# One more 512-column product on TensorE in the first 30 slots of each first attention

## What is computed

```python
def reference(...):
    x = L0_attn_x                                   # (4, 512, 128)
    x = _layernorm(x + _L0_attn_ref(x, ...))        # differential attention, 16 heads of width 8
    x = _layernorm(x + _L0_ffn_ref(x, ...))         # gated feed-forward of width 352, FP4-quantised
    x = _layernorm(x + _L1_attn_ref(x, ...))        # causal attention, 16 query / 4 key heads of width 64
    x = _layernorm(x + _L1_ffn_ref(x, ...))         # one of 8 experts for each token, width 512
    return x
```

```python
a1 = softmax(q1 @ k1.T * scale);  a2 = softmax(q2 @ k2.T * scale)
out = (a1 - lam * a2) @ v
```

## Time and profile before

| | |
|---|---|
| median of 3 runs | 1262.83 us (1258.26 to 1266.27) |
| the profiled execution | 1266.14 us |
| its span, first to last instruction | 1264.3 us |
| mean granted clock of TensorE | 0.843 of 2.4 GHz |
| TensorE (PE), matmuls | 1021.1 us busy, 81% |
| VectorE (DVE) | 786.8 us, 62% |
| ScalarE (ACT) | 641.5 us, 51% |
| GpSimd (POOL) | 424.9 us, 34% |
| DMA | 56.83 MB, 45 GB/s on average |

### The profile page before, as it was taken

One profiled execution on the slowest core, in us unless ns is written; L12 is line 12 of the kernel. 1 busy time (PEld: TensorE's weight loads), 2 busy tenths in 40 slices (PEclk: granted clock), 3 DMA queues, 4 the chain that ended last, 5 costly groups with the idle time before them and its releaser, 6 DMA issues.

```text
span 1264.3 us, 20021 instructions
## 1 busy us (share of the span) xinstructions
PE 1021.1 (81%) x7121; PEld 520.7 (41%) x7121; DVE 786.8 (62%) x1785; ACT 641.5 (51%) x1581; POOL 424.9 (34%) x512
## 2 busy tenths in 40 slices
PE   2588846889999878999988887999988847998754
PEld 1122321233455332455445442355444447455544
DVE  4789347983777678760787667862577562467431
ACT  1177612776266344677167434686257514257423
POOL 3000020300776304000776502200485630487411
PEclk7578955899999875799999775799999968999957
DMA  5300063000013000320103000230100005100052
GB/s 154 96 3 3 10 184 59 2 2 11 0 35 76 1 2 9 125 86 10 31 26 93 1 1 2 83 106 32 32 1 10 1 6 209 32 1 10 1 192 63
DMA packets 54305, 56.83 MB, mean 45 GB/s; under 512 B 13688, under 2 KB 46016, under 8 KB 53440
## 3 DMA queue, kind: packets, MB, share of 16 engines
q1 hardware_dynamic: 53184, 53.47, 14.3%
q0 software_dynamic: 1024, 2.10, 0.6%
HBM read 43.16 MB, written 16.20 MB: 47 GB/s over the span
## 4 chain that ended last, share of the span: by engine, by line
PE 50%; DVE 21%; ACT 10%; issue 8%; POOL 4%; DMA 4%; SPq 3%; POOLq 0%; ACTq 0%; DVEq 0%
PE ps L1583 8%; DVE mx L969 8%; PE ps L1566 5%; PE ps L1612 5%; PE ps L1625 5%; PE ps L1645 4%; PE ps L1655 4%; PE ps L1404 3%; PE ps L1500 3%; ACT PROB L1261 2%; PE ps L1415 2%; PE ps L1398 2%; PE ps L1541 2%; ACT PROB L1303 2%; DMA qst<-mrow 2%
## 5 line engine op out<-in xcount | busy, mean ns | idle before, releaser
L969 DVE TENSOR_REDUCE mx<-ps 128x1 f32<-128x512 f32 x512 | 323.7, 684 | 90.3 <-PE ps L1541 88.1
L1261 ACT ACTIVATE PROB<-ps 128x512 f32<-128x512 f32 x512 | 276.6, 602 | 166.1 <-PE ps L1566 164.4
L577 POOL TENSOR_SCALAR PROB<-PROB,rsum 128x128 f32<-128x128 f32 (+3 forms) x224 | 229.8, 1038 | 72.4 <-DVE rsum L1102 72.0
L1303 ACT ACTIVATE PROB<-ps,mx 128x128 f32<-128x128 f32 (+3 forms) x256 | 133.1, 527 | 165.6 <-DVE mx L1097 163.9
L1583 PE MATMUL ps<-PROB,v 128*32 128x256 f32 x2048 | 184.2, 452 | 3.0 <-ACT OREG L1270 2.6
L1541 PE MATMUL ps<-kst,qst 24*128 24x512 bf16 x512 | 158.9, 477 | 34.1 <-DVE mx L969 26.6
L1566 PE MATMUL ps<-qst,kst 27*128 27x512 bf16 x512 | 142.3, 450 | 39.3 <-ACT PROB L1261 22.8
L558 POOL CAST mparts<-mx 128x16 bf16<-128x16 f32 x32 | 7.0, 218 | 449.4 <-DVE mx L969 427.1
L1097 DVE TENSOR_REDUCE mx<-ps 128x1 f32<-128x128 f32 (+3 forms) x256 | 113.0, 483 | 64.4 <-PE ps L1628 64.2
L1645 PE MATMUL ps<-cst,PROB 128*128 128x128 f32 x640 | 114.2, 298 | 38.5 <-ACT PROB L1318 13.5
L1625 PE MATMUL ps<-MREG,QREG 64*128 64x384 f32 (+3 forms) x512 | 106.9, 495 | 0.0
(11 more groups left out here) (217 smaller groups left out, 1379.6 us busy)
## 6 DMA issues: line engine op xcount, KB each, us to landing
wexp<-expert_rows SPq DMA_DIRECT2D x44, 514.0 KB, 5.2
qk_terms<-RREG SPq DMA_DIRECT2D x48, 128.0 KB, 2.1
kst<-qk_terms SPq DMA_DIRECT2D x16, 192.0 KB
qst<-qk_terms SPq DMA_DIRECT2D x16, 192.0 KB
RREG<-sorted_x SPq DMA_DIRECT2D x4, 704.0 KB, 4.7
sorted_y<-RREG SPq DMA_DIRECT2D x4, 704.0 KB, 3.9
expert_rows<-in_L_ffn_W_dram SPq DMA_DIRECT2D x1, 2048.0 KB
expert_rows<-in_L_ffn_W_dram SPq DMA_DIRECT2D x4, 512.0 KB
```

The source lines that it names most:

```text
L577: pool.tensor_scalar(tile, tile, rsum1[:, 2 * v + half:2 * v + half + 1], None, ALU.mult).then_inc(scaled1, 1)
L969: dve.tensor_reduce(mx0[:, ga % 2, col:col + 1], ps[:, max_bank(k, MAX_SLOT[n]), :], AX, ALU.max, negate=True).then_inc(slot0_free, 1)
L1261: act.activation(prob0[:, s % 2, q % 4, q % 8 // 4], ps[:, s0_banks[q % len(s0_banks)], :], ACT.Exp, scale=float(HD0) ** -0.5).then_inc(ex ...
L1303: act.activation(prob1[:, half, at:at + w], ps[:, a1_bank(v, half), 0:w], ACT.Exp, bias=mx1[:, col:col + 1], accum_out=sum1[:, col:col + 1 ...
```

## The change

TensorE's program gets a helper, called once at the head of each slot of a stretch with a first attention. It issues one bfloat16 product: the identity as weights, 512 columns of the mask table as the moving operand, into bank 7. Nobody reads the result, and no semaphore is incremented. For r = -1 and 0 it does so in slots -8 to 25 (34 slots), for r = 1 and 2 in slots -4 to 25 (30 slots), so 128 times in all. For r = -1 the first of them waits for `rem_ready`, for r = 0 for `hid_done`, since bank 7 is in use before.

```diff
+            def keep_warm(s, c, r):
+                n = 4 * s + c
+                if not (-8 if r <= 0 else -4) <= n < 26:
+                    return
+                if r == 0 and n == -8:
+                    pe.wait_ge(hid_done, NT)
+                if r < 0 and n == -8:
+                    pe.wait_ge(rem_ready, 2)
+                pe.matmul(ps[:, 7, :], identb, pick.rearrange("p a m n -> p (a m n)")[:, 0:T], start=True, stop=True)
+
             def overlap(r):
                 k, i = r + 1, r - 1
                 s0_banks = score_banks(r)
                 ns = len(s0_banks)
                 for s, c in steps(r):
                     if k < BATCH:
+                        keep_warm(s, c, r)
                         if 0 <= s < 16:
                             g = s // 2
```

## The result

| | before | changed |
|---|---|---|
| median of 22 runs | 1265.94 us (1258.26 to 1270.69) | 1269.90 us (1264.90 to 1273.40) |
| span of the profiled execution | 1264.3 us | 1264.9 us |
| mean granted clock in it | 0.843 | 0.866 |

The ratio is 1.0035, with a 95% interval of 1.0024 to 1.0046: slower by 4.4 us (3.0 to 5.8), well within 1%. The forecast was 7.3 us slower. The two profiled executions differ by 0.6 us only; the one of the changed kernel ran in 1266.7 us, 3 us under its median. The runs of the kernel before spread over 12 us and those of the changed one over 9, so single stretches are compared in the profiles and whole times by the ratios.

What follows compares the result with a forecast made beforehand. No single bound: VectorE's maxima pace lead and 2.4 GHz slots, TensorE the 1.2 GHz slots with scores and values. Terms 2.0 - 1.7 + 1.6 + 2.2 + 3.0 + 0.9 - 0.4 - 0.6 + 0.3 = +7.3 us: 1270, range 1254 to 1283.

Steps and rivals of the forecast that it cites:

- The price of a product: On TensorE, per added product: 0.22 to 0.32 us at 2.4 GHz, taken as 0.27; 0.44 to 0.54 at 1.2, taken as 0.50.
- The lead and slots 0 to 5 hidden: Batches 0 and 1, 28 products hidden under VectorE's 1.20 us a slot: cost 0, at most 14 us if cover failed.
- Cold slots 6 and 7: First slots with values at 1.2 GHz, two each in batches 0 and 1: 4 x 0.50 = 2.0 us; 2.05 instead of 1.55 each.
- The clock of batch 0: Clock rises by 68 us and stays up to 95; five slots of batches 0 and 1 turn warm, -1.7 us.
- The warm slots of batches 0 and 1: 30 slots already at 2.4 GHz: product hidden in 0.31 us of slack, except about 6 with two sets of values, 1.6 us.
- The wait for `hid_done`: r = 0, slot -8: VectorE starves 1.1 us, the maxima row's DMA absorbs 1.0; taken as 0.3 us.
- Slots -3 to 0 of batches 2 and 3: Warm and bound by TensorE, one unbroken chain of output and maxima products: 8 x 0.27 = 2.2 us.
- Slots 9 and 11: Batches 2 and 3: with slot 14, three products a batch on the chain after a wait for VectorE, 6 x 0.50 = 3.0 us.
- The last run, half warm: Batches 2 and 3, TensorE's throughout, six slots a batch, half turning warm: 6 x 0.50 - 6 x 0.35 = 0.9 us.
- The reasoning on busy time: Busy time alone doesn't decide TensorE's clock; a whole-array product in each slot should tip unbroken runs of values.
- rival B: Faster: clock held through the whole last run of batches 2 and 3, -6.5 and -5 us; sum -8, 1255 us; chance 0.14.
- Rival A: Products fill TensorE's queue but its clock stays as it was: +17.6 us, so 1280; chance 0.24.

Runs made afterwards that it cites:

- the late products alone: Only the 26 products in slots 13 to 25 of batches 2 and 3, against the kernel before: 0.9961 (0.9935 to 0.9986), -4.9 us.

## Why the prediction was right, and where it was not

The time was forecast at +7.3 us and came at +4.4 (3.0 to 5.8), on the same side and in the range. Step by step:

- *The price of a product*, 0.50 and 0.27 taken out of 0.44 to 0.54 and 0.22 to 0.32. Measured on the chain behind the values: 0.54 and 0.32, the upper bounds, so the weight load adds its 0.10 us there. Behind L1415 in slots -3 to 0: 0.22, the lower bound. Right in kind; what stands in front decides which end holds.
- *The lead and slots 0 to 5 hidden.* Right: +1.4 us for 28, with an interval that includes none. Slots -8 to 0 of batch 0 took 11.23 us for 11.06. The lead of batch 0 kept its pace.
- *Cold slots 6 and 7.* Forecast 2.05 us each. Measured 2.10 and 2.08 from the reduction of slot 6 to that of slot 8, which hold the products of slots 7 and 8. In batch 0 three cold products paid (slots 6, 7 and 8), not two; in batch 1 the same window took 3.32 us for 3.11, at a clock of 0.72 for 0.50.
- *The clock of batch 0.* It was to rise by 68 us; it rose at 72, when L1594 falls to 0.57 us on the chain. Before, it had risen at about 71, so the products didn't bring the rise forward, and slot 8 was not won. The clock stayed up from then on, and slots 14 to 20 went from 9.52 to 8.64 us at 1.00. That the products did this isn't shown: they took 8.63 to 8.66 us at 1.00 also in the profiles of four versions without any product in batch 0, and 9.5 to 10.3 in those of the others.
- *The warm slots of batches 0 and 1*, 6 x 0.27 = 1.6. Right in size. Slots 8 to 14 of batch 0 took 8.41 us, against 7.71 in versions that have no product there and were warm all through; slots 20 to 26 took 8.41 for 8.38.
- *The wait for `hid_done`.* VectorE's idle time was forecast at 1.1 us and is 1.24; slot -9 took 2.95 us for 1.63. That the maxima row's DMA absorbs it was right, as far as a profile shows: from slot -8 to 0 it is 12.55 us in the changed kernel and 15.54 before, with SyncE's queue held by expert loads in both. The first reductions of batch 1's slot -8, by the timeline of the changed kernel (start, duration, engine, line, and in brackets the idle time before them with its releaser):

```profile
199.62 1.89 DVE L969 TENSOR_REDUCE mx<-ps 128x1 f32<-128x512 f32 x3 [1.24 <-PE ps L1541]
```

- *Slots -3 to 0 of batches 2 and 3.* Forecast 1.1 us a batch, measured 0.64 in batch 2 (10.25 for 9.61), three products of 0.22, then 0.22 more to slot 3. Right in kind, a little less in size. In batch 3 the same stretch took 10.25 us for 11.13, since its clock before was only 0.85. That difference goes back to the slots of the lead ahead of it, which have no products.
- *Slots 9 and 11*, in the term of 6 x 0.50. Mis-sized: 1.0 us a batch forecast, 1.95 measured. The step that failed is that each product on the chain adds its price there and the others nothing. I took the stretch for a sum of waits and did not see that GpSimd's two long instructions pace it, and that VectorE had only 1.73 us in batch 2 and 0.43 in batch 3 before it would fall behind one of them.
- *The last run, half warm.* This term was the most mis-sized. With slot 14, L1491 and slot 26 the forecast for slots 13 to 28 was 1.0 + 0.9 - 0.4 - 0.6 = +0.9 us for both batches. Measured: 29.93 + 27.59 against 31.92 + 30.32, so -4.7. Slot 14 itself was right, 0.54 us longer. Half of the run at each level would give a mean of 0.75; the means were 0.78 and 0.90. So in batch 2 the clock was nearly the one forecast and the gain wasn't: what failed there is the price of a warm slot, 0.35 us for its values and scores alone. The run is slots 18 to 26, and most of the gain came in four of them: slots 18, 19, 20 and 26 of batch 2 took 6.68 us for 9.40, 0.68 a slot with the product paid. The forecast had 0.3 for slot 26 and no such gain for the others. The account behind it isn't borne out either: it put the rise down to the whole array being used, and with a quarter of the columns the clock was 0.82 in both.
- *The reasoning on busy time.* Right in what it denied: before, TensorE was busy for 30.51 of 31.92 us with the clock at 0.53, and in the changed kernel for 27.14 of 29.93 at 0.78. The clock rose in a stretch in which the engine's busy share fell.

Two terms were off by more than a microsecond, with opposite signs: slots 8 to 13 (2 x 1.95 for 2 x 1.0, so +1.9) and the last run (-4.7 for +0.9, so -5.6). Together they make -3.7 us, where result and forecast differ by -2.9. So the forecast was close partly by luck, since two errors met. That sum itself is rough: the stretches are of one pair of executions, which differ by 0.6 us, and outside of these stretches the clock rises at other times in them too (slots -13 to -4 of batch 3, with one product at their end, took 21.38 us for 26.21).

One bound in rival B doesn't follow from the prediction's own prices: with 0.35 us for a warm slot and 0.50 for a cold one, "more than nine of the twelve" can't bring the sum below zero; with B's own -11.5 us for twelve some seven would do. No time of the forecast rests on it.

Rival A (only cost) is refuted by the late products alone, 4.9 us faster than before. Rival B (the clock held through the whole last run) is nearly what happened to the clock in batch 3, at 0.90, but the gain there was 2.7 us where B had 5, and batch 2 and slots 8 to 13 kept the kernel from being faster.

## What to carry to other kernels

A filler product on TensorE paid here only where TensorE was the chain at 1.2 GHz for many slots in a row. It cost its streaming time, and behind the values its weight load, wherever TensorE was the chain anyway. Cut such a change by stretch before judging it: here one fifth of the products (26 of 128) gives -5 us and another quarter (34) costs +12. And before a stretch is called bound by one engine's waits, look whether a long instruction of another engine sets where it ends; the same half microsecond, that of slot 11, cost nothing in one version here and set off 1.4 us in another. And look at more than one profile before a rise of the clock is put down to a change: in slots 14 to 20 of batch 0 it came and went without one.

## What the runs showed of the hardware

- A 512-column bfloat16 product over the whole array adds 0.54 us at 1.2 GHz and 0.32 at 2.4 to the chain between 32-column values and 27-row scores. Behind 128-row float32 products its 0.10 us weight load starts while they run, and it adds 0.22 at 2.4 GHz.
- The granted clock was 0.82 in slots 13 to 28 with a product that uses 32 of 128 columns of the array, and 0.78 and 0.90 with one that uses all, against 0.53 and 0.59 without; 0.73 to 0.98 in nine versions with such products and 0.50 to 0.59 in five without.
- The granted clock stayed at 0.50 with TensorE busy for 32.06 of 33.47 us in slots 13 to 28 without an added product, and was 0.90 with it busy for 24.95 of 27.59 us with one in each of slots 13 to 25.
- A VectorE product of two SBUF operands, 0.19 us by itself, took 3.18 us beside a GpSimd instruction of 3.15 us that had started 0.03 us earlier.
